# Three expert blocks instead of five between the last steps of a scan, the other two in the routing behind it

## The reference

```
h = tokens(x)                                   # patches @ W + positions, 2 class tokens in front
h = h + ssm(layernorm(h))                       # scan over the 38 tokens, 16 states per feature
h = h + moe(layernorm(h))                       # 8 experts, top 2: gelu(x @ Wi + bi) @ Wo + bo
h = h + mamba_forward_and_backward(layernorm(h))  # two scans over the tokens
h = h + moe_linear(layernorm(h))                # 8 linear experts, top 2
```

## Time and profile before

| | us |
|---|---|
| median of 3 runs | 951.33 |
| lowest and highest | 948.48, 957.49 |
| the profiled execution | 950.07 |
| its span, from first to last instruction | 948.3 |

### The profile page before, as it was taken

The page is one execution under the profiler, slowest core; times in us unless marked ns, Lnnn a source line. Parts: engine busy times, 40 slices in busy tenths (PEclk is TensorE's granted clock), DMA queues, the critical chain, the costliest instruction groups (busy, mean ns, idle before and its releaser), DMA issues. The chain is left out here.

```text
span 948.3 us, 11720 instructions
## 1 busy us (share of the span) xinstructions
PE 706.7 (75%) x3712; PEld 530.9 (56%) x3712; DVE 564.7 (60%) x968; ACT 404.9 (43%) x880; POOL 394.9 (42%) x311
## 2 busy tenths in 40 slices
PE   7877879585457869997999557777767886776755
PEld 5645546354226769887899334444545554553433
DVE  4167769679765532422122477888887777789430
ACT  1548275375132314332355264564616462644110
POOL 1045745655682322303003243653457433743603
PEclk8999999898677889999999798989977997798687
DMA  9469756355494558799687779797678767976412
GB/s 353 134 210 333 221 153 150 92 135 143 117 257 126 165 166 261 215 281 272 217 240 216 176 188 217 177 235 192 159 199 225 184 151 207 230 188 169 121 31 69
DMA packets 84990, 179.53 MB, mean 189 GB/s; under 512 B 12805, under 2 KB 33153, under 8 KB 84161
## 3 DMA queue, kind: packets, MB, share of 16 engines
q1 hardware_dynamic: 80096, 171.55, 65.7%
q0 software_dynamic: 4832, 7.24, 2.6%
HBM read 158.02 MB, written 20.69 MB: 188 GB/s over the span
## 5 line engine op out<-in xcount | busy, mean ns | idle before, releaser
L1673 PE MATMUL PS<-PR,CM 128*128 128x304 f32 (+1 forms) x672 | 165.3, 434 | 99.7 <-POOL PR L792 69.4
L792 POOL TENSOR_TENSOR PR<-ST,V 128x608 f32<-128x608 f32 x96 | 142.2, 1481 | 184.2 <-DVE ST L1307 165.6
L1673 PEld LDWEIGHTS PS<-PR,CM 128*128 128x128 f32 (+1 forms) x672 | 96.8, 195 | 150.9 <-POOL PR L792 86.5
L958 ACT ACTIVATE dA<-dA,negA 128x304 f32<-128x304 f32 x192 | 93.8, 539 | 156.1 <-DMA BB<-rows_d 155.8
L1307 DVE TENSOR_TENSOR_SCAN ST<-dA,PS 128x608 f32<-128x608 f32 x96 | 136.3, 1420 | 16.9 <-ACT dA L958 12.3
L1010 ACT ACTIVATE HID<-PS,WX 128x128 f32<-128x128 f32 x204 | 59.4, 366 | 144.1 <-PE PS L1673 144.1
L705 POOL TENSOR_TENSOR dA<-dA,aP 128x607 f32<-128x607 f32 x48 | 70.6, 1472 | 75.0 <-ACT aP L978 72.6
L1296 DVE TENSOR_TENSOR PS<-BB,PS 128x608 f32<-128x608 f32 x96 | 76.2, 794 | 23.3 <-DMA BB<-rows_d 12.0
L1673 PE MATMUL PS<-XT,WX 128*128 128x128 f32 x408 | 82.5, 285 | 1.0 <-ACT HID L1010 1.0
L1673 PE MATMUL PS<-WX,HID 128*128 128x192 f32 x408 | 76.6, 339 | 8.6 <-DVE XT L1496 8.6
L1673 PE MATMUL PS<-XT,WXR 128*128 128x128 f32 x408 | 81.2, 282 | 0.0
(11 more groups left out here) (364 smaller groups left out, 1296.2 us busy)
## 6 DMA issues: line engine op xcount, KB each, us to landing
dA<-rows_d SPq DMA_DIRECT2D x144, 304.0 KB, 4.8
BB<-rows_d SPq DMA_DIRECT2D x144, 304.0 KB, 5.5
WX<-ex_m SPq DMA_DIRECT2D x34, 576.0 KB, 4.0
WX<-ex_m SPq DMA_DIRECT2D x34, 387.0 KB, 3.9
slots_d<-WXR SPq DMA_DIRECT2D x8, 960.0 KB, 8.8
WXR<-ex_r SPq DMA_DIRECT2D x34, 192.0 KB, 4.9
WX<-gates_d SPq DMA_DIRECT2D x4, 1216.0 KB, 6.9
CM<-c SPq DMA_DIRECT2D x1, 4430.0 KB, 19.6
```

The lines of the kernel that those rows point to most:

```text
L792: nc.gpsimd.tensor_tensor(PRq[:, c % 2], STq[:, c % 2], DIRS[k].Cw.unsqueeze(1).broadcast_to([128, QB, T]), ALU.mult).then_inc(q_product.s ...
L958: last = nc.scalar.activation(dAq[:, slot, i, :], dAq[:, slot, i, :], ACT.Exp, scale=negA[:, j:j + 1])
L1673: return nc.tensor.matmul(out, lhsT, rhs, start=first, stop=last)
```

## The change

The tables are rewritten: in the last scan the rows of block 0 are turned at step 8 and blocks 0, 1 and 2 stand at steps 9, 10 and 11 (before: turned at step 6, blocks 0 to 4 at steps 7 to 11). Blocks 3 and 4 stand in the routing of group 3, where every step now has a block; before, steps 3 and 6 had none. From step 7 of the routing on, and in the second pass, each step keeps its block. SyncE's full loads of blocks 3 and 4 are written as the routing's loads at steps 0 and 1 in place of the scan's last step.

```diff
-IN_SCAN = {6: -1, 7: 0, 8: 1, 9: 2, 10: 3, 11: 4}
-SCAN_BLOCKS = 5
-IN_ROUTE = {0: 5, 1: 6, 2: 7, 4: 8, 5: 9, 7: 10, 8: 11, 9: 12, 10: 13, 11: 14}
+IN_SCAN = {8: -1, 9: 0, 10: 1, 11: 2}
+SCAN_BLOCKS = 3
+IN_ROUTE = {0: 3, 1: 4, 2: 5, 3: 6, 4: 7, 5: 8, 6: 9, 7: 10, 8: 11, 9: 12, 10: 13, 11: 14}
 IN_PART_A = {0: 15, 1: 16, 2: 17, 3: 18, 4: 19, 5: 20, 6: 21, 8: 22, 9: 23, 10: 24, 11: 25}
...
                             load_narrow(expert_of(2), 2)
-                            load_block(3)
-                            load_block(4)
```

## The result

The median is 936.68 us of four runs (934.94 to 940.51) against 952.15 of four runs of the kernel before (948.48 to 957.49): the ratio of the two kernels is 0.9875 [0.9833, 0.9917], which is 11.9 us of 952.15 (7.9 to 15.9). The two medians alone are 15.5 us apart, near the upper end of that. The forecast was 937, with a gain of 13.3. The profiled execution took 934.94 us, the lowest of the four.

What follows compares the result with a forecast made beforehand. The prediction held that engines wait in turn at the scan's end, VectorE's scan steps behind copies waiting for TensorE, while TensorE is full in the routing. 950.07 - 22.7 + 9.4 = 936.8 us, predicted 937, range 933 to 948.

Steps and rivals of the forecast that it cites:

- the two terms: A gain of 22.7 us at the scan's end and a price of 9.4 us for two more blocks in the routing.
- VectorE's order bounds the scan's end: From scan step 7 VectorE's instructions in order set the pace; step 11 starts at about 304 to 309 us (328.64 before).
- the sum without the clock: Scan's end by VectorE's order with TensorE at full clock: second narrow at 306.19 us, 24.6 us earlier.
- the mark: Start of the second narrow before the scan's last blocks are done: narrow(3) at 330.75 us before, now narrow(1).
- Block 0's row wait is the first and largest loss: At the scan's end TensorE first loses 7.84 us at block 0's turn, waiting for its token rows.
- ScalarE's loads have cover: At the scan's end ScalarE loses six table loads; it has cover, and any part on the path is inside the gain.
- The clock takes 1.9 us: Lowered TensorE clock at blocks 0 and 1 in the scan takes 1.9 us off, leaving a gain of 22.7.
- The price of 9.4: Two blocks added to the routing cost 5.20 us each, 10.4 in all, less a 0.97 us wait.
- The 0.97 us wait: TensorE's wait at narrow(7) in the routing, for a copy queued behind VectorE's scaling, goes away.
- TensorE's wait for its rows stays: In routing step 1 the block behind SyncE's store of the scan's result, now block 5, still waits for its rows.
- Everything behind shifts as a whole: From routing step 7 on everything keeps its order and comes 12 to 15 us earlier.
- The slower rival: Transfers bound the routing: 2.32 us of waiting at all 12 blocks, 27.8 us, time 964.6; chance 0.05.

Runs made afterwards that it cites:

- again: The changed kernel, unaltered, profiled and timed once more: ratio to the kernel before 0.9875, median 941.06 us.
- warm: The changed kernel with 24 filler matmuls, results not read, on TensorE in scan steps 3 to 8: ratio to the kernel before 0.9793, median 932.10 us.
- store_late: The changed kernel with block 5's loads started ahead of the store of the scan's result: ratio to the kernel before 0.9831, median 935.19 us.
- early_turn: The changed kernel with only block 0's turn put back to scan step 6: ratio to the kernel before 0.9934, median 945.49 us.
- No_loads: The kernel before with the exponential in place of the gelu in blocks 0 to 4, avoiding table changes there: ratio 0.9927, median 944.30 us.
- spread: store_late with the weight folding moved from routing step 0 to steps 5, 6 and 7: ratio to the kernel before 0.9785, median 931.22 us.
- before_again: The kernel before, unaltered, profiled once more: 950.5 us in one execution.
- best: spread with warm's filler matmuls added: ratio to the kernel before 0.9797, median 927.93 us.
- after: The changed kernel, three blocks in the scan, against the kernel before: ratio 0.9875, median 936.68 us.

## Why the prediction was right

**The closeness of the time is luck.** The median lies 0.1 us from the sum, but the same kernel in `again` has 941.06, and the sum starts from 950.07 where the four runs of before have 952.15. What is borne out is the two terms, 21.7 for 22.7 and 9.9 for 9.4, and the gain by the ratio, 11.9 for 13.3.

**VectorE's order bounds the scan's end: right, with pieces too short.** Steps 7 and 8 start 2.92 and 5.84 us after the anchor; step 11 starts 28.8 after it, where the forecast of 304 to 309 means 25.8 to 30.8. `gates_top` took 286.18 - 280.91 = 5.27 where 3.96 stood in the sum; two of its instructions ran beside GpSimd's products (one before). The scan of step 10 ends 23.07 us after the anchor, 1.6 later than in the sum (21.48). In warm and store_late, where block 0 runs at full clock, `narrow(0)` waits 1.72 us for VectorE's copy, as the prediction had it, and starts after 23.47 and 23.78 us where the sum without the clock has 22.08. In the changed kernel's own profile TensorE comes last: VectorE waits 0.75 us for block 2's turn, and `narrow(0)` starts after 24.96 us. So of the 24.6 us of the sum without the clock 2.9 were lost, about half to VectorE's longer pieces and half to the clock.

**Block 0's row wait is the first and largest loss: right, and shown.** Early_turn puts it back and loses 10 us at the mark.

**ScalarE's loads have cover: wrong in size.** No_loads shows 2.3 to 3.2 us of path in five loads. They were inside the measured gain, as the prediction said, so the sum is not touched. Four loads fewer are in the program (62 before, 58 now), not six; in the stretch to the mark one stands where five stood:

```profile
286.35 1.28 ACT L1008 ACT_TABLE_LOAD   x1
```

**The clock takes 1.9 us: right in size.** The mean clock of 0.66 and then 0.78 from step 8 to the mark cost 1.4 to 1.7 us there, by warm. It is no fixed cost: store_late's execution did without it. The Trainium skill's "TensorE: Matmul & The Clock Gate", "HAM oscillation — how this bites in real kernels", has bursts behind idle gaps run at half rate; the trace agrees that the clock falls (0.66; 1.00 with the fillers), but here no more than these 1.4 to 1.7 us are on the path, and both `narrow`s before the mark take 2.12 us.

**The price of 9.4: right in sum (9.9), not in its parts.** It is 2.7 for one block and 7.2 for the other, not twice 5.2. The dear one carries 1.6 us of a `narrow` at lowered clock behind a wait for VectorE, which folds weights there; with spread's edits it costs 3.4. Why the first is so cheap no run shows. The 0.97 us wait that the prediction took off is gone, as it said: in the changed kernel no `narrow` from block 3 to block 9 waits for VectorE's copy.

**"TensorE's wait for its rows stays": right.** It is 4.30 us (5.29 before, 4.40 in before_again), and store_late and spread show it could go.

**Everything behind shifts as a whole: not shown.** From `copy_y(9)` to the last `copy_y`, the same program, it takes 149.7 to 150.5 us where it took 145.9 to 147.8. At the last `copy_y` 7.3 to 9.9 of the 11.8 us are left. Since early_turn takes 145.4 for the same stretch and warm 153.5, this can't be put down to the change; the cause is open.

**The slower rival** wanted 1.1 us of waiting at each of the twelve blocks. From 276 to 520 us TensorE waits five times for token rows, 10.9 us in all, and 4.3 of it is the store's. In the kernel before, from 330 to 520 us, it was 10.0 us in four waits, so they have not grown:

```profile
PE PS L1887 <- DMA xp<-slots_d: 10.9, 5, 4.3
```

```profile
PE PS L1889 <- DMA xp<-slots_d: 10.0, 4, 5.3
```

## What to carry to other kernels

An instruction put into an in-order queue ahead of its data stops everything behind it: block 0's turn, at step 6 before its rows, held TensorE, then VectorE, and cost 10 us at the mark without any work; the store ahead of block 5's rows did it again on SyncE. Look for such waits before counting work, and move the issue, not only the work. When two profiles differ more than the change can, find the last instruction that both share and count from there.

## What the runs showed of the hardware

- Scan step 6, up to which the program is the same but for the fillers of warm and best, started between 273.74 and 281.02 us in fourteen profiles, a spread of 7 us that is as large as the effects studied.
- Two VectorE instructions of 102x24 elements took 1.33 and 1.49 us (281.31 and 283.32) where the same two operations took 0.18 at 285.06 in this profile and at 299.07 in before; each ended with a product of GpSimd's (1.47 us each, from 281.14 and 283.31). The Trainium skill's "SBUF — State Buffer", "Who interferes with whom", says that a VectorE instruction with two SBUF inputs contends with a GpSimd instruction that reads SBUF; the trace agrees.
- TensorE can be busy 9.47 of 10.70 us at a mean clock of 0.66: a full engine is not yet one at full speed. Filler matmuls raised the clock to 1.00 and moved the mark by 1.4 to 1.7 us; what they are worth in the whole time is open. The same code ran block 0's matmuls at 0.63 us a pair in one execution and at 0.39 in another (after, store_late).
